# Cross-attention of a decoder layer: one pass with a running maximum, or two passes with the maxima taken first

## The chip, the core and the metric

The kernel runs on one core of a Trainium2 chip. The metric is the device time of one execution in microseconds. TensorE multiplies matrices, VectorE (DVE) and ScalarE (ACT) work on rows, GpSimd (POOL) copies and fills, and SyncE (SP) issues most of the DMA transfers. The engines run their own instruction streams and meet at semaphores.

## What is computed

One decoder layer, cut to what matters here (H = 16 heads of 32, D = 512, 4 batches of 128 queries, 2048 keys each):

```python
q = (layernorm(x) @ Wq.T + bq); k, v = ctx @ Wkv.T + bkv
scores = einsum('bthd,bshd->bhts', q, k * 32 ** -0.5) + attn_bias + where(mask, 0, -inf)
x = x + (softmax(scores) @ v) @ Wo.T + bo            # cross-attention
x = x + self_attention(layernorm(x))                 # clamped
x = x + expert_layer(layernorm(x))                   # 8 experts, 32 rows each and batch
```

The mask lets a query see only keys near the end of the 2048, so most of the 64 chunks of 128 keys are masked as a whole.

## The kernel before, in words

**Which chunks.** A chunk is worked on if its mask has an open key, or if it is the last of its batch. A small table made on the chip lists them; with these inputs it has 11 (four last ones and seven others). Loops with a counter in a register (`Fori`) run over the table, and `chunk_j` and `chunk_b` read its chunk and its batch.

**Prologue.** SP loads x, Wq (`wq_s`), Wk, the first chunk and Wv; ACT loads the rest. Every weight except Wk is split in a rounded part `w_hi` (a copy on ACT) and the remainder `w_lo` (a subtraction on DVE, `split_att`), and a product is three matmuls (hi by hi, hi by lo, lo by hi). The rows of layernorm(x) are turned (`turn_batch`) and split in `tr_hi`, `tr_lo`; `project_t` (L1193) makes the queries `qt` of all batches.

**A chunk** (`chunk`, `softmax_chunk`, with the turned context chunk in `ctx_s`): `k_project` (L1167, 16 full-precision products, in the trace 32 matmuls) makes turned keys in PSUM bank `pk`, DVE adds the bias into `kt_s`. `scores` (L1243, L1248) puts the key bias in the four banks `ps` and adds query by key for 16 heads, four heads side by side in strips of 32 rows. DVE takes the row maxima (L824, two halves) and combines them with those of the chunks before; ACT takes the exponentials (L449, one instruction a head, as each head has its own maximum, with the row sums beside it). TensorE turns the 16 blocks of probabilities (`turn_probs`, L1255), DVE and ACT copy them to `big_b`, `values` (L1268) multiplies by the values, ACT copies the result, TensorE turns it back (`turn_values`, L1276), and DVE rescales `state` and adds. `v_project` (L1177, 12 matmuls) makes the next chunk's values between these steps: chunk t+1's keys, values and scores are made while chunk t is in its softmax.

**Afterwards.** The four batches' results are divided by their row sums, turned, and projected by Wo (`cross_project`, L1193); then come layernorm, self-attention (`project_half`, L1193, begins its queries), the gate, and eight experts, which fill the second half. The change does not touch the experts.

Of the kernel before, what the change touches and what calls it, by code (L numbers as in the profile page):

```python
# [6 lines left out]
ALU = mybir.AluOpType  # L7
# [5 lines left out]
I32 = mybir.dt.int32  # L13
# [23 lines left out]
def decoder_layer(nc, x, ctx_t, key_bias, key_mask, wq, bq, wk, bk, wv, bv, wo, bo,  # L37
                  sq, sbq, sk, sbk, sv, sbv, so, sbo, gate, w1, w2, out):
    with ExitStack() as ctx:
# [11 lines left out]
        ot_s = att_w[:, 6, 0].rearrange("p (k t) -> p k t", k=KC)  # L51
# [5 lines left out]
        ctx_hi, ctx_lo = w_hi[:, 0, :, 0:P], w_lo[:, 0, :, 0:P]  # L57

        x_s = sb("x_s", [P, B, D])
        norm = sb("norm", [P, B, D])  # L60
        gcol = sb("gcol", [P, E])
        qk = sb("qk", [P, 2, B, KC, T])
        qt, kt2 = qk[:, 0], qk[:, 1]
        tr_gate = qt
        state = sb("state", [P, B, D])
        total = sb("total", [P, B, H])
        neg_max = sb("neg_max", [P, B, H])
        sums = sb("sums", [P, H])
# [8 lines left out]
        negm = sb("negm", [P, H])  # L77
        mdiff = sb("mdiff", [P, H])
        alpha = sb("alpha", [P, H])
        norm_c = sb("norm_c", [P, B, H])  # L80
# [5 lines left out]
        table = sb("table", [1, 2 * (NJ + 1) + 2], I32)  # L86
# [11 lines left out]

        tr_hi = early("tr_hi", [P, KC, B * T], F32R)
        tr_lo = early("tr_lo", [P, KC, B * T], F32R)  # L100
        big_a = early("big_a", [P, H, P])
        ctx_s = early("ctx_s", [P, KC, P])
# [4 lines left out]
        values.close()  # L107
        onehot_s = early("onehot_s", [P, B * E * CAP], F32R)
# [12 lines left out]
        kb_m = first("kb_m", [NJ, P])  # L121
        kb_3 = first("kb_3", [NJ, 3, P], BF16)
# [4 lines left out]
        start.close()  # L127
        big_b = early("big_b", [P, H, P])
# [22 lines left out]
        of_group = ctx_s[:, 3].rearrange("p (g m) -> p g m", g=KC)  # L151
# [21 lines left out]
        in_mask, in_wk, in_wv, in_bo, in_sb, in_gate, in_cols = (sem(f"in_{n}") for n in (  # L173
            "mask", "wk", "wv", "bo", "sb", "gate", "cols"))
# [3 lines left out]
        rows_out = sem("rows_out")  # L178
        consts = sem("consts")
        act_ok = sem("act_ok"); place_mm = sem("place_mm")  # L180
        pick_ok = sem("pick_ok"); table_mm = sem("table_mm"); table_ok = sem("table_ok"); rows_ok = sem("rows_ok")
# [32 lines left out]


        TURN_BANKS = [[0, 1, 2, 3], [4, 4, 0, 7], [5, 4, 1, 2], [4] * 4, [1, 2, 3, 1]]
        V2_BANKS = [3, 0, 1, 4]
        CROSS_BANKS = [5, 4, 1, 2]

        def turned(i, b):  # L220
# [1396 lines left out]
```

## Time and profile before

| | us |
|---|---|
| three timed runs | 471.87, 472.13, 474.87 (median 472.13) |
| profiled execution, from its first to its last instruction (its span) | 470.1 |
| first query projection starts | 19.17 |
| scores of chunk 0 start | 32.6 |
| loop over chunks, one turn | 11.6 |
| scores of the last chunk start | 152.0 |
| self-attention queries start (`project_half`) | 179.77 |
| experts start | 261.3 |

No time of its own is given for the profiled execution; its span is 2.0 us under the median of the timed runs, and what lies around the span is in that difference. Times are read from the start of the span. A matmul's end is modelled, so its pace is read from start to start.

### The profile page before, as it was taken

The numbers are of one execution on the slowest core, as the hardware profiler recorded it, in microseconds if no ns is written. First come the engines' busy times: TensorE is split into PE (matmuls) and PEld (weight loads), VectorE is DVE, ScalarE is ACT, GpSimd is POOL, SyncE is SP. The second block draws the span as 40 slices with busy tenths as digits, with TensorE's granted clock in tenths as the row PEclk, the third lists the DMA queues.
The fourth block names the chain that finished last, engine by engine and source line by source line (L and its number), as shares of the span: only waits on it lengthen the run. The fifth ranks groups of instructions, "written<-read, shape, count | busy, mean of one in ns | idle before, by whom it ended". The sixth has DMA issues, their size and how long they took to land.

```text
span 470.1 us, 9681 instructions
## 1 busy us (share of the span) xinstructions
PE 437.7 (93%) x3345; PEld 361.9 (77%) x3345; DVE 371.1 (79%) x513; ACT 295.9 (63%) x609; POOL 79.0 (17%) x89
## 2 busy tenths in 40 slices
PE   1989999999998999989997999999999999999993
PEld 1868888888887779868875877877878787878782
DVE  5986777777778886749887999898989898998853
ACT  1536666666665743466323887777777878787742
POOL 5000000000000013000014250504132230505000
PEclk9999999999999999999999999999999999999998
DMA  7991010000000552520000099999999989998002
GB/s 255 276 342 55 24 24 23 23 23 23 23 23 2 199 205 91 176 93 3 3 1 0 14 392 388 386 386 387 373 345 342 358 305 354 311 386 274 0 0 89
DMA packets 42959, 81.99 MB, mean 174 GB/s; under 512 B 3000, under 2 KB 3128, under 8 KB 42936
## 3 DMA queue, kind: packets, MB, share of 16 engines
q1 hardware_dynamic: 38744, 75.85, 45.6%
q10 hardware_dynamic: 4192, 5.83, 4.0%
q8 instruction: 14, 0.23, 0.2%
q14 instruction: 9, 0.07, 0.0%
HBM read 80.58 MB, written 1.10 MB: 174 GB/s over the span
## 4 chain that ended last, share of the span: by engine, by line
PE 72%; DVE 11%; ACT 9%; DMA 4%; issue 2%; SPq 1%; POOL 0%; DVEq 0%
PE po L1501 19%; PE pk L1501 10%; PE pv L1501 10%; PE pv L1177 6%; ACT big_a L449 5%; PE ps L1193 5%; PE ps L1255 3%; PE pv L1193 3%; PE po L1527 3%; DVE mc L824 3%; PE ps L1248 2%; DMA att_w<-in_wq 2%; PE po L1276 1%; PE pk L1193 1%; DMA rows<-kb 1%
## 5 line engine op out<-in xcount | busy, mean ns | idle before, releaser
L1122 DVE TENSOR_TENSOR w_lo<-att_w,w_hi 128x2048 fp32r<-128x2048 f32 x60 | 137.9, 2306 | 21.6 <-ACT w_hi L643 21.6
L643 ACT CAST w_hi<-att_w 128x2048 fp32r<-128x2048 f32 x60 | 114.9, 1915 | 15.6 <-PE po L1501 15.6
L449 ACT ACTIVATE big_a<-ps,negm 128x128 f32<-128x128 f32 x176 | 62.5, 407 | 21.1 <-DVE negm L827 21.1
L1501 PE MATMUL po<-w_hi,ht_hi 128*128 128x512 f32 x128 | 52.2, 408 | 0.0
L1501 PE MATMUL po<-w_hi,ht_lo 128*128 128x512 f32 x128 | 50.5, 395 | 0.0
L1501 PE MATMUL po<-w_lo,ht_hi 128*128 128x512 f32 x128 | 50.3, 393 | 0.0
L449 ACT ACTIVATION_READ_ACCUMULATOR big_a<-ps,negm 128x1 f32 x176 | 43.4, 247 | 0.0
L1167 PE MATMUL pk<-ctx_s,att_w 128*128 128x128 f32 x352 | 42.5, 279 | 0.4 <-DMA ctx_s<-in_ctx_t 0.4
L1167 PEld LDWEIGHTS pk<-ctx_s,att_w 128*128 128x128 f32 x352 | 40.6, 193 | 2.7 <-issue 1.8
L824 DVE TENSOR_REDUCE mc<-ps 128x8 f32<-128x1024 f32 x22 | 26.9, 1221 | 12.4 <-PE ps L1248 12.4
L1501 PEld LDWEIGHTS po<-w_hi,ht_lo 128*128 128x128 f32 x128 | 24.0, 188 | 6.1
L1501 PEld LDWEIGHTS po<-w_lo,ht_hi 128*128 128x128 f32 x128 | 24.1, 188 | 5.1
L1501 PEld LDWEIGHTS po<-w_hi,ht_hi 128*128 128x128 f32 x128 | 24.1, 188 | 4.9
L387 POOL COPY q_now<-qk 128x512 f32 x10 | 6.3, 626 | 123.8 <-PE ps L1248 123.8
L1501 PE MATMUL pk<-w_hi,xin_hi 128*128 128x512 f32 x64 | 26.3, 411 | 0.0
L1501 PE MATMUL pv<-w_hi,xin_hi 128*128 128x512 f32 x64 | 26.2, 409 | 0.0
L1501 PE MATMUL pk<-w_hi,xin_lo 128*128 128x512 f32 x64 | 25.3, 395 | 0.0
L1501 PE MATMUL pk<-w_lo,xin_hi 128*128 128x512 f32 x64 | 25.2, 394 | 0.0
L1501 PE MATMUL pv<-w_hi,xin_lo 128*128 128x512 f32 x64 | 25.1, 393 | 0.0
L1501 PE MATMUL pv<-w_lo,xin_hi 128*128 128x512 f32 x64 | 25.1, 393 | 0.0
L420 POOL CAST back_now<-state 128x128 fp32r (+1 forms) x8 | 8.6, 1069 | 94.7 <-PE ps L1548 87.8
L1255 PEld LDWEIGHTS ps<-ident,big_a 128*128 128x128 f32 x176 | 21.1, 140 | 4.3
(300 smaller groups left out, 990.9 us busy)
## 6 DMA issues: line engine op xcount, KB each, us to landing
att_w<-in_w SPq DMA_DIRECT2D x64, 1024.0 KB, 6.9
ctx_s<-in_ctx_t SPq DMA_DIRECT2D x11, 256.0 KB, 2.6
x_s<-in_x SPq DMA_DIRECT2D x4, 256.0 KB, 3.4
att_w<-in_wq SPq DMA_DIRECT2D x1, 1024.0 KB, 8.3
att_w<-in_wk SPq DMA_DIRECT2D x1, 1024.0 KB, 11.1
att_w<-in_wv SPq DMA_DIRECT2D x1, 1024.0 KB, 6.2
att_w<-in_sv ACTq DMA_DIRECT2D x1, 1024.0 KB, 8.3
att_w<-in_wo ACTq DMA_DIRECT2D x1, 1024.0 KB, 10.3
```

The source lines that it names most:

```text
L420: g.tensor_copy(back_now[:], back[:, bass.ds(e, 1), :].rearrange("p a n -> p (a n)")).then_inc(back_staged, 1)
L449: ins = a.activation(big_a[:, h], ps[:, c, g * P:(g + 1) * P], ACT.Exp, bias=negm[:, h:h + 1], accum_out=sums[:, h:h + 1])
L643: a.copy(w_hi[:, i % SLOTS], att_w[:, i]).then_inc(hi_ok, 1)
L824: v.tensor_reduce(mc[:, hs], ps[:, 2 * half:2 * half + 2].rearrange("p c (g k) -> p (c g) k", k=P), AX.X, ALU.max).then_inc(loop_dve, 1)
L1122: v.tensor_tensor(w_lo[:, i % SLOTS], att_w[:, i], w_hi[:, i % SLOTS], ALU.subtract).then_inc(lo_ok, 1)
L1167: ins = mm(pk[:, g * P:(g + 1) * P], wk_s[:, k, g * P:(g + 1) * P], ctx_s[:, k], start=k == 0, stop=k == KC - 1)
L1177: ins = mm(pv[:], c[:, k], w[:, 1, k], start=k == 0 and c is ctx_hi and w is w_hi, stop=k == KC - 1 and c is ctx_lo, skip_group_check=True)
L1193: ins = mm(dst, l, r, start=n == 0, stop=n == len(pairs) - 1, skip_group_check=True)
L1248: ins = mm(ps[:, c, g * P:(g + 1) * P], q_now[r, g], kt_s[r, g], start=False, stop=True, skip_group_check=True)
L1255: ins = nc.tensor.transpose(ps[:, c, g * P:(g + 1) * P], big_a[:, c * KC + g], ident[:])
L1501: ins = mm(dst, l, r, start=start and i == 0, stop=i == len(terms) - 1, skip_group_check=True)
L1527: ins = nc.tensor.transpose(po[:, 1, c * P:(c + 1) * P], h_s[:, q % 2, c * P:(c + 1) * P], ident[:])
```

## The change

1. The maxima come first. Each batch's last chunk is known without the table: its context is loaded early to `ctx_last`, its keys are made early (`last_keys`) and stay in SBUF (`kt_last`), and its scores' maxima are taken before the loops. Then a first loop over the other chunks (n = 7) makes keys, scores and maxima only. It writes each chunk's keys to DRAM (`kept_kt`).
2. The maxima are placed in rows (`shift_rows`), turned by TensorE and kept as `neg_t`.
3. A second loop reads the keys back, makes the scores turned (keys on the rows, `scores_t`) with the maximum already subtracted, and takes four exponentials of 512 columns with the key bias as a column `kb_now`. Probabilities come out in the layout that `values` needs, so that `turn_probs`, `turn_values`, the rescaling and their copies are gone. Row sums are matmuls with `of_group` beside the values.
4. After the second loop each batch's last chunk follows, and the row sums are inverted and spread by matmuls (`spread_cross`), as self-attention does.
5. The keys' bias is added on ACT (`keys_out`), `ctx_k` and `bias3` are copies of what is loaded, Wk and the first batch's last chunk are loaded ahead of Wq, Wo and the others are loaded by SP, and the biases come in one transfer.

The core of the diff (cut; lines of TensorE, ACT and DVE):

```diff
         @block.scalar
+            act.wait_ge(in_cols, 16)
+            last_keys(0)
             split_att(0)
             for b in range(B):
                 transposed(0, b)
...
+            with act.Fori(0, n) as t:
+                act.wait_ge(kept, t * 16 + 16)
+                act.wait_ge(k_mm, 2 * t + 1)
+                keys_out(kt_s, pk, 0, 2).then_inc(k_out, 1)
+                act.wait_ge(k_mm, 2 * t + 2)
+                keys_out(kt_s, pv, 2, 4).then_inc(k_out, 1)
+                act.wait_ge(k_out, 2 * t + 2)
+                act.dma_start(kept_kt[bass.ds(t, 1)].rearrange("a p (k n) -> (a p) k n", k=KC), kt_s[:]).then_inc(kept, 16)
...
         @block.vector
+            def lower(nm, i):
...
+                v.tensor_reduce(mc[:], ps[:].rearrange("p c (g k) -> p (c g) k", k=P), AX.X, ALU.max).then_inc(max_ok, 1)
+                dve.wait_ge(max_ok, 2 * i + 1)
+                v.scalar_tensor_tensor(nm, mc[:], -1.0, nm, ALU.mult, ALU.min).then_inc(max_ok, 1)
+            for b in range(B):
+                dve.wait_ge(sl_mm, b + 1)
+                lower(neg_max[:, b], b)
+                if b == 1:
+                    split_att(2)
...
         @block.tensor
+            with pe.Fori(0, n) as t:
+                pe.wait_ge(ctx_k_ok, t + 1)
+                k_project(pk, ctx_k, 0, 2).then_inc(k_mm, 1)
+                k_project(pv, ctx_k, 2, 4).then_inc(k_mm, 1)
+                pe.wait_ge(bias_ok, t + 1)
+                pe.wait_ge(q_staged, t + 1)
+                pe.wait_ge(max_ok, 2 * t + (2 * B - 1))
+                pe.wait_ge(k_out, 2 * t + 1)
+                scores(bias3, q_now, kt_s, 2 * t + 2).then_inc(s_mm, 1)
...
+            with pe.Fori(0, n) as t:
+                pe.wait_ge(kt_in, t * 16 + 16)
+                pe.wait_ge(staged2, 2 * t + 2)
+                pe.wait_ge(p_ok, t + 1)
+                scores_t(neg_now, q_now, kt_s).then_inc(st_mm, 1)
+                pe.wait_ge(ctx_lo_ok, t + 2)
+                pe.wait_ge(v_out, t + 1)
+                v_project(pv[:], 0).then_inc(v_mm, 1)
+                pe.wait_ge(p_ok, t + 2)
+                pe.wait_ge(acc_ok, t + 1)
+                values(0).then_inc(pv_mm, 1)
```

TensorE, the turn of a chunk in the loop before: `pk` holds keys, `pv` values, `ps` scores and turned probabilities, `po` the output; of the twelve value matmuls the first three stand for all.

```order
L1255 MATMUL ps<-ident,big_a 128x128 [waits p_ok]
L1255 MATMUL ps<-ident,big_a 128x128 x3
L1177 MATMUL pv<-w_hi 128x512
L1177 MATMUL pv<-w_lo,w_hi 128x512
L1177 MATMUL pv<-w_hi,w_lo 128x512
...
L1243 MATMUL ps<-bias,ones 128x512 [waits pt_act,pt_dve]
L1243 MATMUL ps<-bias,ones 128x512 x3
L1248 MATMUL ps<-kt_s,q_now 128x128 x16
```

and what stands in the first and in the second loop now:

```order
L1229 MATMUL pk<-ctx_k,att_w 128x128 [waits ctx_k_ok]
L1229 MATMUL pk<-ctx_k,att_w 128x128 x7
L1229 MATMUL pv<-ctx_k,att_w 128x128 x8
L1363 ISA [waits q_staged,bias_ok]
L1364 REGISTER_ALU [waits max_ok]
...
L1295 MATMUL ps<-kt_s,q_now 128x128 x8
...
L1295 MATMUL ps<-kt_s,q_now 128x128 [waits k_out]
...
L1312 MATMUL ps<-neg_now,ones 128x512 [waits p_ok]
L1312 MATMUL ps<-neg_now,ones 128x512 x3
L1316 MATMUL ps<-q_now,kt_s 128x128 x16
```

The turns of probabilities are gone; scores stand twice, and the first loop's end with a wait for keys.

DVE ahead of the first loop, in the changed kernel (`ps` is the one set of score banks, `x_s` the rows of x, `ctx_k` the copy that TensorE's first loop waits for); before, DVE had no such row, since a chunk's maxima stood beside TensorE's next projections:

```order
L852 TENSOR_TENSOR w_lo<-big_a,w_hi 128x4x128 [waits cl_hi_ok] x2
L855 TENSOR_TENSOR x_s<-x_s,bo_b 128x512 [waits in_rows]
L855 TENSOR_TENSOR x_s<-x_s,bo_b 128x512 x3
L867 TENSOR_REDUCE mc<-ps 128x16 [waits sl_mm,dchain]
L869 SCALAR_TENSOR_TENSOR neg_max<-mc,neg_max 128x16 [waits max_ok]
...
L808 TENSOR_TENSOR w_lo<-att_w,w_hi 128x2048 [waits att_hi_ok]
...
L880 COPY ctx_k<-ctx_s 128x512 [waits ctx1_in,kept]
```

Four reductions, each behind scores in the same banks, now stand between TensorE's last scores and its first loop. ACT's start, in the changed kernel (`qk` takes the keys of the first last chunk):

```order
L538 ACT_TABLE_LOAD [waits kl_mm]
L538 ACTIVATE qk<-pk,cols 128x128 [waits in_cols]
L538 ACTIVATE qk<-pk,cols 128x128 x3
L524 CAST w_hi<-att_w 128x2048 [waits in_wq]
L528 CAST tr_hi<-ps 128x4x128 [waits tr_mm0] x4
```

The table load and the split of Wq moved behind the wait for the first keys' matmuls (`kl_mm`).

## Rows read from the trace of the kernel before

**Rows 1.** The page, busy time of each engine and share of the span.

```profile
PE 437.7 (93%) x3345; PEld 361.9 (77%) x3345; DVE 371.1 (79%) x513; ACT 295.9 (63%) x609; POOL 79.0 (17%) x89
```

**Rows 2.** Timeline of TensorE: start, duration, what [idle before it and releaser].

```profile
38.25 3.73 PE L1167 MATMUL pk<-ctx_s,att_w 128*128 128x128 f32 x32
41.73 0.48 PE L1177 MATMUL pv<-w_hi 128*128 128x512 f32 x1
...
46.59 0.40 PE L1243 MATMUL ps<-bias,ones 32*128 32x512 bf16 x4
...
47.80 1.08 PE L1268 MATMUL po<-big_b,v_s 128*32 128x128 f32 x32
48.81 3.84 PE L1167 MATMUL pk<-ctx_s,att_w 128*128 128x128 f32 x32
52.95 0.66 PE L1276 MATMUL po<-ident,att_w 128*128 128x128 f32 x4 [0.30 <-ACT att_w L460]
...
58.20 0.40 PE L1243 MATMUL ps<-bias,ones 32*128 32x512 bf16 x4
```

**Rows 3.** Windows after TensorE's wait at 30.7; the last but two column: granted clock.

```profile
32.60:34.60 2.00, 2.00 (x37) 1.77 (x38) 1.98 (x1) 0.00 (x0) 0.00 (x0) 0.63 1.05 406
34.60:36.40 1.80, 1.80 (x5) 1.41 (x6) 1.64 (x4) 0.00 (x0) 0.72 (x1) 0.50 0.99 331
```

**Rows 4.** Timeline of TensorE, the waits and starts outside the loop.

```profile
19.17 0.48 PE L1193 MATMUL ps<-tr_hi,w_hi 128*128 128x512 f32 x1
...
30.26 0.40 PE L1193 MATMUL ps<-tr_lo,w_hi 128*128 128x512 f32 x1
32.58 0.40 PE L1243 MATMUL ps<-bias,ones 32*128 32x512 bf16 x4 [1.93 <-DMA bias<-rows]
...
179.77 0.36 PE L1193 MATMUL pk<-tr_hi,w_hi 128*128 128x256 f32 x1
...
207.16 1.17 PE L1365 MATMUL ps<-qk 32*128 32x128 f32 x32 [1.33 <-DVE qk L972]
```

**Rows 5.** Timeline of TensorE: a projection of 12 matmuls, spread sums, values with sums.

```profile
156.42 0.48 PE L1193 MATMUL pv<-w_hi,tr_hi 128*128 128x512 f32 x1
...
159.29 1.03 PE L1255 MATMUL ps<-ident,big_a 128*128 128x128 f32 x8
...
226.17 1.05 PE L1394 MATMUL po<-kt_s,q_now 128*128 128x128 f32 x8
227.15 0.43 PE L1383 MATMUL po<-big_b,v_s 128*32 128x128 f32 x8
...
229.03 0.50 PE L1193 MATMUL pv<-w_hi,tr_hi 128*128 128x512 f32 x1
```

**Rows 6.** Groups by line on DVE and ACT: busy us, mean ns | idle before.

```profile
L824 DVE TENSOR_REDUCE mc<-ps 128x8 f32<-128x1024 f32 x22 | 26.9, 1221 | 12.4 <-PE ps L1248 12.4
L721 DVE TENSOR_TENSOR w_lo<-att_w,w_hi 128x2048 fp32r<-128x2048 f32 x7 | 16.0, 2286 | 2.5 <-ACT w_hi L438 2.5
L841 DVE TENSOR_TENSOR state<-state,alpha 128x512 f32 x11 | 7.5, 684 | 0.1
L987 DVE RECIPROCAL kt_s<-po 128x128 f32<-128x128 f32 x2 | 1.9, 954 | 0.2 <-PE po L1386 0.2
...
L449 ACT ACTIVATE big_a<-ps,negm 128x128 f32<-128x128 f32 x176 | 62.5, 407 | 21.1 <-DVE negm L827 21.1
...
L549 ACT ACTIVATE qk<-po,cols 128x512 f32<-128x512 f32 x2 | 1.4, 690 | 1.5 <-PE po L1193 1.5
```

**Rows 7.** Timeline of ACT at the start.

```profile
4.74 1.28 ACT L438 ACT_TABLE_LOAD   x1 [4.74 <-issue]
11.12 1.90 ACT L438 CAST w_hi<-att_w 128x2048 fp32r<-128x2048 f32 x1 [5.09 <-DMA att_w<-in_wq]
```

**Rows 8.** DMA issues: KB each, median us from issue to landing.

```profile
ctx_s<-in_ctx_t SPq DMA_DIRECT2D x11, 256.0 KB, 2.6
...
rows<-kb SPq DMA_DIRECT2D x1, 48.0 KB, 5.8
```

More of the change, by code:

```diff
@@ new lines, in last_keys, with split_last, exponents @@
+            def last_keys(b):
+                act.wait_ge(kl_mm, b + 1)
+                keys_out(kt_last[:, b], pk, 0, KC).then_inc(kl_out, 1)
+            def split_last(b):
+                act.wait_ge(in_last, 48)
+                a.copy(ctx_part(w_hi, b), ctx_last[:, b]).then_inc(cl_hi_ok, 1)
+            def exponents(bias):
+                for c in range(STRIPS):
+                    ins = a.activation(big_a[:, c * KC:(c + 1) * KC].rearrange("p g n -> p (g n)"), ps[:, c], ACT.Exp, bias=bias)
+                return ins
@@ new lines, in scores @@
+            def scores(rows, queries, keys, waits):
+                for c in range(STRIPS):
+                    r = slice(c * DH, (c + 1) * DH)
+                    mm(ps[:, c].rearrange("p (g k) -> p g k", g=KC), ones3[r], rows[r].unsqueeze(1).broadcast_to([DH, KC, P]),
+                       start=True, stop=False, skip_group_check=True)
+                for g in range(KC):
+                    if g == 2 and waits is not None:
+                        pe.wait_ge(k_out, waits)
+                    for c in range(STRIPS):
+                        r = slice(c * DH, (c + 1) * DH)
+                        ins = mm(ps[:, c, g * P:(g + 1) * P], queries[r, g], keys[r, g], start=False, stop=True, skip_group_check=True)
+                return ins
@@ new lines, in last_scores, with scores_t @@
+            def last_scores(b):
+                pe.wait_ge(kl_out, b + 1)
+                if b == 0:
+                    pe.wait_ge(bias_last_in, 64)
+                    pe.wait_ge(q_out, KC)
+                else:
+                    pe.wait_ge(max_ok, 2 * b - 1)
+                scores(bias_last[:, b], qt[:, b], kt_last[:, b], None).then_inc(sl_mm, 1)
+            def scores_t(rows, queries, keys):
+                for c in range(STRIPS):
+                    r = slice(c * DH, (c + 1) * DH)
+                    mm(ps[:, c], ones3[r], rows[r], start=True, stop=False, skip_group_check=True)
+                for g in range(KC):
+                    for c in range(STRIPS):
+                        r = slice(c * DH, (c + 1) * DH)
+                        ins = mm(ps[:, c, g * P:(g + 1) * P], keys[r, g], queries[r, g], start=False, stop=True, skip_group_check=True)
+                return ins
@@ L1224, in _ @@
+            pe.wait_ge(consts, 10)
+            pe.wait_ge(in_wk, 16)
+            last_keys(0)
+            for b in range(B):
+                turn_batch(0, b)
+            pe.wait_ge(act_ok, 1)
+            mm(pv[0:NJ, 0:1], tri[:], idx[:, 7:8], start=True, stop=True).then_inc(table_mm, 1)
+            last_keys(1)
+            pe.wait_ge(tr_lo_ok[0], B)
+            pe.wait_ge(att_lo_ok, 1)
+            project_t(2, banks[0:4], q_mm)
             pe.wait_ge(pick_ok, 1)
@@ L1297, in _ @@
-            for b in range(B):
-                turn_batch(0, b)
-            pe.wait_ge(in_wk, 16)
-            k_project(0)
-            pe.wait_ge(tr_lo_ok[0], B)
-            pe.wait_ge(att_lo_ok, 1)
-            project_t(2, banks[0:4], q_mm)
-            pe.wait_ge(q_out, 4)
-            scores(0)
-            pe.wait_ge(att_lo_ok, 2)
-            for k in range(KC):
-                v_project(0, k)
-            chunk(0, False)
-            with pe.Fori(1, prev) as t:
-                chunk(t, True)
@@ L1350, in _ @@
             pe.wait_ge(tr_lo_ok[2], B)
-            project_half(1, banks[4:8], 1, q2_mm)
+            project_half(1, q2_dst, 1, q2_mm)
             pe.wait_ge(v2_out, B - 1)
```

830 lines of the change are left out of this document (431 added, 399 removed).

## The prediction

> **What bounds the kernel now.** I read the page of the profile first: TensorE is busy 93% of the span [rows 1]. Then its timeline in the loop over chunks. From the scores at 46.59 to the next at 58.20 are 11.61 us [rows 2], and TensorE's only recorded wait there is 0.30, for ACT's copy of the last output; by starts it is more, since 32 key matmuls started at 38.25 let the next group start at 41.73, so 3.48 us after, while those of 48.81 are followed at 52.95 only: 0.66 us lost a turn. I take 0.2 more as lost before the scores, where the turned probabilities must first be copied from the same banks. So TensorE's own work is 10.7 of 11.6 us, and no change of the softmax can gain more than 0.9 us a chunk unless it takes work from TensorE. Outside the loop TensorE waited 1.93 us for the key bias at 30.7 [rows 4], and afterwards its clock was granted at 0.63 and then 0.50 of full speed until 36.4 [rows 3]: of its two levels the lower, 1.2 GHz, for some 3.8 us, in which half the work is done: 1.9 us lost. A wait of 1.33 at 205.8 [rows 4] had no such cost.
>
> **TensorE's work, old and new.** Prices from start to start: keys 3.48, scores 1.21 (46.59 to 47.80), values 1.01 [rows 2]; a projection of 12 matmuls 2.87, a spread of sums 0.98, values with sums 1.88 [rows 5]. The change removes 16 turns of probabilities (about 1.5, by the rest of the 11.61) and four turns of the output (0.4), makes the scores twice (+1.21) and adds the sums to the values (+0.87). A chunk costs 3.48 + 1.21 + 2.87 + 1.21 + 1.88 = 10.65, as before. What it can gain are the loop's waits; what it can lose are new waits where one loop became a prologue, two loops, a middle and a closing part. I follow TensorE through them.
>
> **Prologue, up to the queries.** The first keys need Wk and a chunk, as many bytes as went before Wq's landing at 11.1 [rows 7]; the four column loads and a broadcast that ran beside are gone, so I take 10.3 (9.5 to 11.1). The first products run at the low clock, 3.48 + 1.9: keys done at 15.7. ACT, which before had split Wq from 11.1, now stands behind them: a table load of 1.28, then of 4 x 0.27 + 0.1 = 1.2 for the keys (four 128-column activations; 407 ns each [rows 6], issued faster), then the split of 1.90 [rows 7], to 20.3 with handovers. DVE's remainder takes 2.29 and four turned remainders 2.5 (0.68 each alone, some 0.6 in a row [rows 6]): the query projection starts at 25.2, against 19.17 [rows 4]. TensorE has turned x and made the second keys by 22.0 and waits 3.2 us. It then takes 11.3 (30.26 + 0.23 less 19.17) + 1.9 for the clock: 38.4.
>
> **Prologue, up to the first loop.** Scores of batch 0 wait for the last queries on ACT: 39.4 to 40.6. Nine small instructions of DVE for the table hold TensorE till 40.9; third keys till 44.4. DVE meanwhile does two remainders (1.3) and adds bo to x (four, 2.5), and only then the maxima: 2048 columns cost twice 1.22 less one start, 2.3 [rows 6], to 47.0. The scores' banks are free then: a wait of 2.6. At the low clock those scores take 2.4, to 49.5, and the fourth keys end at 53.7 (0.7 late); scores to 54.9. DVE reduces and splits the third weight in between, and reduces batch 2 till 57.4: a wait of 2.6, slow scores to 59.9. Then the first loop waits for the last reduction and the copy to ctx_k: 0.25 + 2.3 + 0.2 + 0.5, to 63.2, a wait of 3.3.
>
> **First loop.** Keys 3.48; their last result is out 0.25 later, ACT needs 0.27 + 0.37 and two handovers for the second half, so the second half of the scores starts at 4.55 and ends at 5.1. DVE's 0.4 + 0.2 + 2.3 + 0.2 and POOL's copy fit beside. Behind ACT's wait for `kept` stands the first half of the keys' copy. It is not waited for if the DRAM write lands within 3.5 us of its issue (5.1 + 3.48 less 4.55 and the copy). 256 KB in the other direction land in 2.6, 48 KB of `rows` took 5.8 behind other loads [rows 8]; I take the nearer row, 2.6, and keep 5.8, by which a turn is 7.0 and the time 12 more, for the range. Seven turns of 5.1 and 1.9 for the clock: 100.8. The Trainium skill (DMA: Bandwidth & Descriptors, Anatomy of one DMA) says that completion can take surprisingly long when the target is HBM; the trace of before has no unhindered write of this size in the loop to test it. By the page's fit of 2.0 us and 436 GB/s I get, as an estimate, 2.6 us and an unchanged sum.
>
> **Between the loops.** Three value projections 8.6, 16 turns of 0.41 are 1.65, a wait of 0.95 for DVE (last maximum, 19 small instructions, a remainder, two copies of 0.68), and 0.9 for the keys read back, whose load is queued behind three weights of 1 MB: 12.1, to 112.9.
>
> **Second loop.** 1.21 + 2.87 + 1.88 = 5.96, I take 6.0. ACT's four exponentials (0.69 each alone [rows 6], 2.2 together) end 2.5 after the scores, under the 2.87 of the projection; DVE's copy of the values ends 0.95 after the values, under the next scores' 1.21. Seven turns: 42.0, to 154.9. Both loops together give 11.1 a chunk, 0.5 less than before: 3.6 us gained.
>
> **Closing part.** TensorE's work up to `project_half`: 4 scores 4.8, a projection 2.9, 4 values 7.5, 4 spreads 3.9, 4 + 2 projections 17.2, 3 turns 1.2: 37.6. Its waits, by DVE's order, are 1.05 and 0.55 for the first sums (0.9 to add, 0.95 for the reciprocal [rows 6]), 0.6 for batch 1's remainder, 2.0 before batch 2's projection (scale, ACT copy, remainder), 1.0 for batch 3's reciprocal, 1.3 for the remainder of the queries' weight: 6.5. So 44.1, to 199.0 (179.77 before [rows 4]): +19.2. Self-attention's rest and the experts keep their order and their loads are early enough, at 0; in the worst case later loads of Wsq would add a few us, which I do not expect. So span 489.3, and with the 2.0 between span and median 491.3. I take 490, as one of the four slow stretches may not come or may be shorter.
>
> **The clock.** Rows 3 and 4 show that 1.93 us of waiting were enough. The new waits at 22.0, 44.4, 54.9 and 59.9 are 3.2, 2.6, 2.6 and 3.3, longer. They cost 1.9 + (1.2 + 0.7) + 1.2 + 1.9 = 6.9. The Trainium skill (TensorE: Matmul & The Clock Gate, What's actually happening) calls the lower rate the default that activity lifts, with a phase that is not the kernel's; whether each wait is caught is then not settled by its length alone. The trace agrees for the wait it has.
>
> **Rivals.** (A) The waits come, but the clock stays up at all four. For it: 1.33 us did nothing; against it: 1.93 did. 490 - 6 = 484. (B) The DRAM write sets the first loop, as priced: 490 + 12 = 502; half of it, with a landing at 4.6, gives 495. Against it: the queue is empty there but for 256 KB a turn. (C) Faster: TensorE is never kept waiting, in prologue, middle or closing part, and its work alone sets the end. That takes away 3.2 + 1.0 + 0.3 + 2.6 + 2.6 + 3.3 + 0.95 + 0.9 + 6.5 = 21.4 and the 6.9 of the clock: 463. It decides at the reductions: if DVE's 2.3 us were hidden under a projection, as before, it would be so; against it, there is one set of score banks and the next scores stand behind the reduction. For half of it, 476. (D) The small instructions and handovers, which I estimated, are 10% dearer everywhere: 494; this lies in the range of the first.
>
> **How the numbers follow.** All four stretches or three of them slow, 490: 0.68 (its own range 484 to 496). A, 484 (479 to 486): 0.18. B, 502 or part of it: 0.08. C, or enough of it for no loss: 0.06, of it 0.04 faster by over 1%, under 467.4, and 0.02 within 1%. About 1% of 472.13, 4.7 us, is what a measurement of this kernel can tell from no change. A is above 476.9, so it is slower. Slower is 0.68 + 0.18 + 0.08 = 0.94; I give 0.03 of it to the same for a sum of small errors: slower 0.91, same 0.05, faster 0.04. The range from 479 to 498 leaves out C and the worse half of B.
>
> **What would show it.** The changed profile should have: queries' projection starting near 25 with a table load of 1.3 after the first keys; three waits of 2.5 to 3.3 on TensorE for L867 or L880, each followed by a granted clock of 0.5; a first loop of 5.1 a turn with no wait for DMA; a second of 6.0; DVE's and ACT's busy time lower; `project_half` near 197 to 199; then 290 us as before. The prediction is wrong if the first loop waits for `kept`, if the second is set by ACT or DVE, or if the stage between the last scores and `project_half` is hidden.

## The result, and the profile after

The changed kernel takes 496.95 us (median of 4 runs, 492.29 to 498.92), the kernel before 472.66 in the runs beside it: a ratio of 1.051, 95% interval 1.0469 to 1.0551, so slower by 5%. The forecast was 490 with a range from 479 to 498, so the median lies 1 us inside the upper end, and one run in four outside it. The profiled execution took 498.92, and its span is 497.2, where the forecast had a span of 489.3.

The page of the changed kernel, busy time of each engine (answers to [rows 1]):

```profile
PE 450.0 (91%) x3906; PEld 373.0 (75%) x3906; DVE 338.5 (68%) x422; ACT 264.1 (53%) x319; POOL 93.2 (19%) x116
```

DVE has 32.6 us less to do and ACT 31.8, and the time is longer all the same. TensorE is busy for 12.3 us more, most of it work at half rate. This is what a share of busy time can't tell: the two engines that were relieved were not the ones that ended last.

TensorE's waits, engine and line waited for, then total us, times, longest:

```profile
PE ps L1288 <- DVE mc L867: 4.7, 2, 2.5
PE pk L1229 <- DVE ctx_k L880: 3.9, 1, 3.9
PE ps L1312 <- DMA kt_s<-kept_kt: 3.1, 1, 3.1
PE ps L1248 <- DVE tr_lo L802: 2.6, 1, 2.6
```

The first is made of 2.18 at 46.7 and 2.52 at 56.8, the two reductions that stand between one set of scores and the next. All were forecast, as 2.6 twice, 3.3, 0.9 and 3.2. The windows in which TensorE's clock was low (windows of the changed kernel; busy time of each engine, then the granted clock, the last but two column; answers to [rows 3]):

```profile
26.50:32.70 6.20, 6.16 (x15) 4.80 (x16) 2.65 (x3) 2.02 (x4) 0.00 (x0) 0.50 0.27 103
48.90:53.60 4.70, 4.69 (x52) 4.48 (x53) 3.16 (x4) 0.00 (x0) 0.00 (x0) 0.64 0.01 3
64.80:70.30 5.50, 5.49 (x25) 5.49 (x26) 0.06 (x1) 0.63 (x2) 0.00 (x0) 0.50 0.19 48
118.00:121.00 3.00, 3.00 (x38) 2.63 (x39) 0.51 (x1) 0.70 (x2) 0.56 (x2) 0.52 0.31 91
265.00:268.50 3.50, 3.50 (x9) 2.79 (x10) 2.03 (x5) 0.00 (x0) 0.55 (x1) 0.53 0.00 0
```

0.50 is the lower of the two levels, 1.2 GHz. Each window follows a wait, and costs its length times what is missing to 1.00: 3.1, 1.7, 2.7, 1.4 and 1.6 us. The fourth runs on a little, to 121.5. A short stretch behind the wait that ends at 59.29 (0.73 from 59.3 to 61.0) costs 0.5 more. The last lies in the part that the change does not touch, behind 16 recorded matmuls of 8 columns, four of 128 and a wait of 0.50 us.

A turn of each loop, from TensorE's timeline (start, duration; answers to [rows 2]):

```profile
77.84 2.05 PE L1229 MATMUL pk<-ctx_k,att_w 128*128 128x128 f32 x16
79.73 1.95 PE L1229 MATMUL pv<-ctx_k,att_w 128*128 128x128 f32 x16
81.64 0.39 PE L1288 MATMUL ps<-bias,ones 32*128 32x512 bf16 x4
81.87 1.26 PE L1295 MATMUL ps<-kt_s,q_now 32*128 32x128 f32 x32
83.06 2.05 PE L1229 MATMUL pk<-ctx_k,att_w 128*128 128x128 f32 x16
...
125.60 0.39 PE L1312 MATMUL ps<-neg_now,ones 32*128 32x512 bf16 x4
125.82 1.06 PE L1316 MATMUL ps<-q_now,kt_s 32*128 32x128 f32 x32
129.76 0.43 PE L1323 MATMUL po<-big_a,v_s 128*32 128x128 f32 x8
...
131.64 0.39 PE L1312 MATMUL ps<-neg_now,ones 32*128 32x512 bf16 x4
```

The first loop turns in 83.06 - 77.84 = 5.22 us, the second in 131.64 - 125.60 = 6.04. Together 11.26, against 11.61 before: 0.35 a chunk gained, in a loop whose softmax is gone.

The rest of the milestones, from TensorE's timeline, with the waits in brackets (answers to [rows 4]):

```profile
11.78 5.68 PE L1229 MATMUL pk<-big_a,att_w 128*128 128x128 f32 x32 [11.78 <-DMA big_a<-in_ctx_t]
...
26.54 0.79 PE L1248 MATMUL ps<-tr_hi,w_hi 128*128 128x512 f32 x1 [2.61 <-DVE tr_lo L802]
...
41.68 0.40 PE L1288 MATMUL ps<-bias_last,ones 32*128 32x512 bf16 x4 [0.32 <-ACT qk L583]
...
64.81 3.78 PE L1229 MATMUL pk<-ctx_k,att_w 128*128 128x128 f32 x16 [3.88 <-DVE ctx_k L880]
...
117.98 0.55 PE L1312 MATMUL ps<-neg_now,ones 32*128 32x512 bf16 x4 [3.12 <-DMA kt_s<-kept_kt]
...
190.36 0.50 PE L1248 MATMUL ps<-w_hi,tr_hi 128*128 128x512 f32 x1 [1.72 <-DVE tr_lo L979]
...
205.60 0.38 PE L1248 MATMUL pk<-tr_hi,w_hi 128*128 128x256 f32 x1 [1.06 <-DVE w_lo L808]
```

The last of these rows is `project_half`, at 179.77 before. The change costs 25.8 us up to there, and 1.3 behind it (497.2 - 205.6 against 470.1 - 179.77), which the 1.6 of the window at 265 covers. So four questions were open: is it the waits, and each of them for the reason that I had read; is it the clock, and does the clock follow the waits; how near was the DRAM write to setting the first loop; and do the waits account for everything, so that a kernel without them is no slower than before?

### The profile page after: what moved, and what is told of

It is laid out like the page before. It is cut to its first block, busy times and chain, and to the rows that moved or that the text cites. A ratio compares the mean times of both kernels' runs of the same rounds, so it can differ in the third digit from the quotient of the medians.

```text
span 497.2 us, 10365 instructions
## 1 busy us (share of the span) xinstructions
PE 450.0 (91%) x3906; PEld 373.0 (75%) x3906; DVE 338.5 (68%) x422; ACT 264.1 (53%) x319; POOL 93.2 (19%) x116
## 4 chain that ended last, share of the span: by engine, by line
PE 79%; DVE 11%; DMA 3%; ACT 3%; issue 2%; SPq 1%; DVEq 0%; POOL 0%; ACTq 0%
PE po L1621 18%; PE pv L1248 9%; PE pk L1621 9%; PE pv L1621 9%; PE ps L1248 6%; PE pk L1229 5%; PE po L1647 3%; PE pv L1229 2%; PE po L1323 2%; PE ps L1295 2%; PE ps L1316 2%; DVE mc L867 2%; PE po L1326 2%; DMA big_a<-in_ctx_t 2%; PE pk L1248 1%
## 5 line engine op out<-in xcount | busy, mean ns | idle before, releaser
L1229 PE MATMUL pk<-big_a,att_w 128*128 128x128 f32 x128 | 18.5, 313 | 12.5 <-DMA big_a<-in_ctx_t 11.8
L867 DVE TENSOR_REDUCE mc<-ps 128x16 f32<-128x2048 f32 x11 | 25.2, 2290 | 4.8 <-PE ps L1295 4.8
L1229 PEld LDWEIGHTS pk<-big_a,att_w 128*128 128x128 f32 x128 | 17.8, 227 | 12.9 <-issue 12.8
L552 ACT ACTIVATE big_a<-ps,kb_now 128x512 f32<-128x512 f32 x28 | 17.0, 689 | 17.3 <-PE ps L1316 17.3
L1621 PE MATMUL pv<-w_hi,xin_lo 128*128 128x512 f32 x64 | 25.2, 394 | 0.0
L929 DVE TENSOR_TENSOR w_lo<-ctx_s,w_hi 128x512 fp32r<-128x512 f32 x9 | 6.2, 692 | 26.9 <-ACT w_hi L560 26.9
L500 POOL COPY x_now<-qk 128x512 f32 x7 | 16.2, 2308 | 38.3 <-PE pv L1621 38.3
L503 POOL TENSOR_TENSOR xin_lo<-x_now,xin_hi 128x512 fp32r<-128x512 f32 x7 | 23.0, 3288 | 0.6
```

Source lines behind the costliest of these rows:

```text
L500: g.tensor_copy(x_now[:], now).then_inc(x_now_ok, 1)
L503: g.tensor_tensor(xin_lo[:], x_now[:], xin_hi[:], ALU.subtract).then_inc(xin_staged, 1)
L552: ins = a.activation(big_a[:, c * KC:(c + 1) * KC].rearrange("p g n -> p (g n)"), ps[:, c], ACT.Exp, bias=bias)
L867: v.tensor_reduce(mc[:], ps[:].rearrange("p c (g k) -> p (c g) k", k=P), AX.X, ALU.max).then_inc(max_ok, 1)
L1229: ins = mm(dst[:, g * P:(g + 1) * P], wk_s[:, k, g * P:(g + 1) * P], chunk[:, k], start=k == 0, stop=k == KC - 1)
L1621: ins = mm(dst, l, r, start=start and i == 0, stop=i == len(terms) - 1, skip_group_check=True)
```

## The experiments

**Keeping TensorE busy in its waits.** Nothing is moved; matmuls that nobody reads stand in the waits.

```diff
+            def keep_busy(n):
+                for _ in range(n):
+                    mm(po[:, 0, 0:P], ident[:], ident[:], start=True, stop=True, skip_group_check=True)
...
             last_keys(1)
+            keep_busy(9)
             pe.wait_ge(tr_lo_ok[0], B)
...
             last_keys(2)
+            keep_busy(7)
             last_scores(1)
             last_keys(3)
             last_scores(2)
+            keep_busy(8)
             last_scores(3)
+            keep_busy(14)
...
             pe.wait_ge(neg_t_ok, B)
+            keep_busy(11)
             with pe.Fori(0, n) as t:
```

> The changed kernel, with 9, 7, 8, 14 and 11 matmuls that nobody reads (128x128 of the identity by itself, into a bank that is free) where TensorE waits 2.61, 2.18, 2.52, 3.88 and 3.12 us. If the waits bring the low clock (my account), the granted clock stays at 1.0 to the end of the first turn of the second loop, and the time falls by what the slow stretches lost: 3.1 from 26.5 to 32.7, 1.7 from 49 to 54, 0.4 at 59.3, 2.6 from 64.8 to 70 and 1.6 from 118 to 121, so 9.4: some 487.5. The runs should also lie closer together than 492.3 to 498.9. Rival: the clock falls for a reason that is not the waits (a rhythm of its own, or the load); then the slow stretches stay, and the time is 497 or somewhat more, since surplus matmuls then delay the next group.

Measured: 489.12 us (487.58 to 490.18), ratio 1.0342 (1.0285 to 1.0398), 7.8 less than the changed kernel. Its windows where the clock had been low:

```profile
26.10:38.40 12.30, 12.01 (x55) 9.37 (x55) 3.03 (x6) 4.27 (x8) 0.00 (x0) 1.00 0.15 56
45.70:50.60 4.90, 4.89 (x68) 4.75 (x68) 3.58 (x4) 0.00 (x0) 0.00 (x0) 1.00 0.00 0
54.40:63.40 9.00, 8.35 (x96) 7.98 (x96) 3.15 (x5) 0.62 (x2) 0.00 (x0) 1.00 0.13 30
110.40:113.40 3.00, 2.93 (x44) 2.53 (x45) 0.08 (x1) 1.57 (x3) 1.17 (x2) 1.00 0.39 107
```

All at 1.00, and the runs lie within 2.6 us of each other where the changed kernel's spread over 6.6; the mean granted clock of the four is 0.989 to 0.996, that of the changed kernel's four 0.965 to 0.977. `project_half` starts at 196.50, 9.1 earlier, against 9.4 expected. More work, less time: the clock follows the waits, and cost the changed kernel some 8 of its 24 us.

**The same in the kernel before.** Eight such matmuls in its wait of 1.93 us.

```diff
             project_t(2, banks[0:4], q_mm)
+            keep_busy(8)
             pe.wait_ge(q_out, 4)
             scores(0)
```

> The kernel before, with 8 matmuls that nobody reads in its wait of 1.93 us at 30.7. By my account of the clock the granted clock then stays at 1.0 from 32.6 to 36.4 and the time from the first scores to the loop's first falls from 14.0 to 12.1: 471 where the kernel before has 473. Rival: the low clock there has nothing to do with the wait, and the stretch stays at 14.0.

Measured: 472.07 (10 runs), ratio 0.999 (0.9961 to 1.0019). The mechanism came as expected, the gain did not. In its profile the clock is 1.00 where it was 0.57, and from the first scores, at 33.99, to the loop's first, at 46.41, are 12.4 us, not 14.0:

```profile
32.11 1.95 PE L1223 MATMUL po<-ident 128*128 128x128 f32 x16
33.99 0.39 PE L1247 MATMUL ps<-bias,ones 32*128 32x512 bf16 x4
...
46.41 0.40 PE L1247 MATMUL ps<-bias,ones 32*128 32x512 bf16 x4
```

But the unread matmuls last to the very start of the scores, and the profile shows no wait behind them; in this execution the projection also ended 1.6 us later than in [rows 4]. How much of the 1.6 us they gave back by lasting too long the profile can't say. In the medians 0.5 us of gain is left, and the interval goes from 1.8 us less to 0.9 more, so that the 2 us expected are all but excluded and a smaller gain is not. This execution also has a slow stretch that the one of [rows 3] doesn't, from 250 to 254 us (0.57), behind a wait of 1.45 in the part that nobody changed. So the control shows the link between wait and clock a second time, and that filler of the wait's full length is worth nothing that these runs can tell; that it must end sooner is a reading of this profile, and wasn't tried.

**The first chunk's copies ahead of the last reduction.**

```diff
             for b in range(B):
+                if b == B - 1:
+                    dve.wait_ge(kept, 16)
+                    dve.wait_ge(ctx1_in, 16)
+                    next_chunk().then_inc(ctx_k_ok, 1)
+                    dve.wait_ge(bias_in, 64)
+                    next_bias().then_inc(bias_ok, 1)
                 dve.wait_ge(sl_mm, b + 1)
                 lower(neg_max[:, b], b)
```

> The changed kernel, with the copies of the first chunk and its bias (ctx_k, bias3) ahead of the fourth reduction on DVE instead of behind it. If the wait of 3.88 us ahead of the first loop is DVE's order alone, the keys of the loop start right behind the last scores: 3.9 less, and the 2.6 that the low clock cost in the first turn come back as well where the clock doesn't fall at 59.3 already; between 3.9 and 6.5 less, 491 to 493. Rival: the chunk's load or its bias (over DRAM) is what is late there, and the copy was only next to it: then the wait stays in another place and the time is within 1 us of 497.

Measured: 490.76 (489.3 to 493.75), ratio 1.0393 (1.0328 to 1.0458): 6.2 less, in the upper half of what was expected. The wait is gone (TensorE's timeline; the keys of the first loop now follow the last scores):

```profile
56.45 0.40 PE L1289 MATMUL ps<-bias_last,ones 32*128 32x512 bf16 x4 [2.51 <-DVE mc L867]
...
57.96 3.37 PE L1230 MATMUL pk<-ctx_k,att_w 128*128 128x128 f32 x16
...
63.05 0.40 PE L1289 MATMUL ps<-bias,ones 32*128 32x512 bf16 x4
```

From the fourth last scores to the loop's first are 6.6 us, against 11.9 in the changed kernel (59.29 to 71.19). There DVE had (timeline of the changed kernel):

```profile
60.99 2.29 DVE L867 TENSOR_REDUCE mc<-ps 128x16 f32<-128x2048 f32 x1 [1.64 <-PE ps L1295]
63.32 0.17 DVE L869 SCALAR_TENSOR_TENSOR neg_max<-mc,neg_max 128x16 f32<-128x16 f32 x1
64.33 0.43 DVE L880 COPY ctx_k<-ctx_s 128x512 f32<-128x512 f32 x1 [0.84 <-issue]
```

So the 3.9 us were one instruction of 0.43 us standing behind one of 2.29 (and 0.84 of `issue`, where DVE by its order reads the number of turns), on an engine that is busy for 68% of the span.

**The weights' loads behind the second loop.**

```diff
             load_chunk(first_j, ctx2_in)
-            load_att(sq_s, sq, in_sq)
-            load_att(sk_s, sk, in_sk)
-            load_att(so_s, so, in_so)
-            sp.dma_start(gate_s[:], ...).then_inc(in_gate, 16)
...
+            load_att(sq_s, sq, in_sq)
+            load_att(sk_s, sk, in_sk)
+            load_att(so_s, so, in_so)
+            sp.dma_start(gate_s[:], ...).then_inc(in_gate, 16)
             sp.wait_ge(v_out, n + 2)
```

> The changed kernel, with the loads of the three weights of 1 MB and of the gate behind the second loop on SP's queue, not ahead of its first read of keys. If the keys' first read was late because it stood behind 3 MB, the wait of 3.12 us ahead of the second loop falls to under 0.6 and its slow clock (1.6) goes: 4 less, 493. Rival: the read waits for the end of the last write to DRAM and for the copy of V's chunk, not for the queue; then the wait stays over 2 us. A second rival: the weights, now issued near 157, come late in the closing part (the split at 195), which would show as a wait for DMA there and cost up to 5.

Measured: 493.71 (490.53 to 497.17), ratio 1.046 (1.0397 to 1.0523), 3.2 less in the median. The runs overlap with those of the changed kernel, so the stage is the better witness: from the turned maxima to the second loop's first scores are 5.9 us (105.67 to 111.61) against 8.5 (109.49 to 117.98), and the loop behind them takes 42.4 against 43.9. That is 4.1, as expected. The first read of the keys, issued behind the weights at 112.64, took 5.1 us to its landing in the changed kernel; here it is issued at 108.83 and takes 2.4. Where it was late there is now this:

```profile
111.61 0.40 PE L1312 MATMUL ps<-neg_now,ones 32*128 32x512 bf16 x4 [0.56 <-POOL neg_now L474]
```

The closing part takes 43.74 us, as before the move (43.72), so the weights, issued some 45 us later, still come in time.

**DVE's additions early.**

```diff
             split_att(1)
+            for b in range(2, B):
+                dve.wait_ge(cl_hi_ok, b - 1)
+                v.tensor_tensor(ctx_part(w_lo, b), ...).then_inc(cl_lo_ok, 1)
+            dve.wait_ge(in_rows, 32)
+            for b in range(B):
+                ins = v.tensor_tensor(x_s[:, b], x_s[:, b], bo_b[:], ALU.add)
+            link(ins)
             dve.wait_ge(table_mm, 2)
```

(and away from behind the table)

> The changed kernel, with DVE's two remainders of the last chunks and the four additions of bo (3.75 us) put into its idle time of 12 us before 41.2, ahead of the table. Then the first reduction starts at 42.9 instead of 46.5 and ends before the next scores are due: TensorE's wait of 2.18 goes, and so does the slow stretch from 49 to 54: 2.2 + 1.7 = 3.9 less, 493. Rival: DVE's split of the third weight, which stands between the second and the third reduction, takes the place of the first one as what is late, so that the later waits grow by what is gained: within 1 us of 497.

Measured: 491.32 (490.76 to 496.28), ratio 1.0415 (1.0339 to 1.0491), 5.6 less, more than expected. The wait of 2.18 is gone, and from the first last scores to the first loop are 20.2 us (37.68 to 57.85) against 23.1: 2.9, less than the 3.9 forecast for it. What came on top is in part a chance of the clock. The same wait of 2.6 us stands ahead of the query projection as before, but here the clock did not fall:

```profile
25.30:31.30 6.00, 5.95 (x26) 4.81 (x27) 5.91 (x9) 2.20 (x5) 0.00 (x0) 1.00 0.37 139
```

**Wq first.** The order of the kernel before at the start.

```diff
+            load_att(wq_s, wq, in_wq)
             load_att(wk_s, wk, in_wk)
             load_last(0)
-            load_att(wq_s, wq, in_wq)
...
-            last_keys(0)
             split_att(0)
             for b in range(B):
                 transposed(0, b)
-            last_keys(1)
+            last_keys(0)
             split_att(1)
...
-            pe.wait_ge(in_wk, 16)
-            last_keys(0)
             for b in range(B):
                 turn_batch(0, b)
...
-            last_keys(1)
+            pe.wait_ge(in_wk, 16)
+            last_keys(0)
             pe.wait_ge(tr_lo_ok[0], B)
             pe.wait_ge(att_lo_ok, 1)
             project_t(2, banks[0:4], q_mm)
...
-            nc.tensor.transpose(pk[:, 0:NJ], kb_m[:], ...)
+            nc.tensor.transpose(po[:, 0, 0:NJ], kb_m[:], ...)
+            last_keys(1)
             last_scores(0)
```

> The changed kernel with the order of the kernel before at its start: Wq is loaded ahead of Wk and the first last chunk, ACT splits it before it touches keys, TensorE turns x before the first keys, and the second keys come behind the query projection. If the keys put ahead of Wq are what made the start late, the query projection starts at 19 to 20, as before, and the scores of batch 0 at 35 to 36, not at 41.7: 6 less, 491. Rival: Wk and the chunk, now behind Wq, come so late that the first keys hold the projection; then it starts at 21 or more and the gain is under 4.

Measured: 484.9 (484.55 to 489.69), ratio 1.0301 (1.0243 to 1.0358): 12.0 less, twice what was expected. TensorE's timeline:

```profile
18.39 0.51 PE L1248 MATMUL ps<-tr_hi,w_hi 128*128 128x512 f32 x1 [0.71 <-DVE tr_lo L802]
...
34.10 0.40 PE L1288 MATMUL ps<-bias_last,ones 32*128 32x512 bf16 x4
35.50 3.81 PE L1229 MATMUL pk<-big_a,att_w 128*128 128x128 f32 x32
39.24 0.39 PE L1288 MATMUL ps<-bias_last,ones 32*128 32x512 bf16 x4
```

The projection starts at 18.39, and the first last scores 7.6 us earlier, since the wait of 2.6 ahead of the projection is 0.7 and its slow stretch is gone. The rest is what I had not counted: the second keys now lie between the projection and the first scores, and DVE makes its additions beside them; the second last scores follow the third keys with no wait (39.24), so that the 2.18 and its slow stretch are gone as well.

**How near the DRAM write is.** Less of it, and twice as much:

```diff
-    act.dma_start(kept_kt[...], kt_s[:]).then_inc(kept, 16)
+    act.dma_start(kept_kt[...][:, 0:1], kt_s[:, 0:1]).then_inc(kept, 16)
```

> The changed kernel, where only the first quarter of each chunk's keys (64 KB, not 256) is written to DRAM and read back; three quarters of the keys of the second loop are left out, with the same instructions. In the changed kernel ACT waits 3.7 to 3.8 us of every turn of the first loop for the write, and copies the keys 0.06 us before the scores want them. If the write doesn't set the loop, its turn stays at 5.21 and only ACT's wait shrinks. If it does (the rival), the turn falls to 5.0 or less.

```diff
     act.dma_start(kept_kt[...], kt_s[:]).then_inc(kept, 16)
+    act.dma_start(kept_kt2[...], kt_s[:]).then_inc(kept, 16)
```

> The changed kernel, where each chunk's keys are written to DRAM twice, into two places (512 KB a turn). The write now lands 3.6 to 4.3 us after its issue, with at most 0.2 us to spare by my reading. Then every 0.1 us of later landing shows: I expect a landing some 0.6 to 1.2 later and a turn of 5.7 to 6.3, 3.5 to 7.5 us more in all. Rival: there is slack of over 1 us (as I had forecast less than 1), and the turn stays under 5.3.

The first of them leaves out three quarters of the second loop's keys, so that it tells about the first loop's pace alone. Measured, one run each, 493.56 and 497.63 us; a single run says little, and the turns are read from the traces. The groups of transfers by KB and us to landing, of the changed kernel and then of the smaller write:

```profile
kept_kt<-kt_s ACTq DMA_DIRECT2D x7, 256.0 KB, 3.6
kt_s<-kept_kt SPq DMA_DIRECT2D x7, 256.0 KB, 2.5
```

```profile
kept_kt<-kt_s ACTq DMA_DIRECT2D x7, 64.0 KB, 2.8
kt_s<-kept_kt SPq DMA_DIRECT2D x7, 64.0 KB, 1.8
```

With the small write the turn is 5.21 (80.12 to 85.33), as in the changed kernel, and ACT waits again for TensorE. So the write doesn't set the loop. But it just doesn't, as ACT's row in the changed kernel shows:

```profile
80.96 0.62 ACT L538 ACTIVATE kt_s<-pk,cols 128x128 f32<-128x128 f32 x2 [3.83 <-DMA kept_kt<-kt_s]
```

The copy ends at 81.58, and the scores that read it start at 81.64; in the turn where it ends latest, at 92.14, they start at 92.20, and that turn still takes 5.21 (88.27 to 93.48). With two writes the starts of the turns are 68.62, 74.34, 79.55, 85.39, 90.60 and 96.35: every other turn takes 5.7 to 5.8, and the mean is (96.35 - 68.62) / 5 = 5.55, 0.34 more. That is less than the 0.5 to 1.1 I expected, and more than the rival's, so both were off: there is some slack, of a few tenths, and then the write shows.

**The four moves together.** Wq first, the copies first, the read first, the additions early.

> The changed kernel with the four moves that each gained by themselves: Wq first at the start, DVE's additions early, the first chunk's copies ahead of the fourth reduction, the weights' loads behind the second loop. If the gains are of different waits and add up: from 484.9 (Wq first alone) the wait ahead of the first loop goes (3.9) with some 1.0 of its slow clock, and the wait ahead of the second falls by 2.2 with 1.0 of slow clock: 476.8, between 475 and 479. The wait of 2.5 between the third and the fourth last scores must stay, since TensorE has nothing there. Rival: waits grow elsewhere on DVE, which is as long as before in this stretch: then 480 or more.

Measured: 479.55 (477.12 to 481.77), ratio 1.0166 (1.0121 to 1.0211), 0.6 above the range from 475 to 479, and under the rival's 480. The profiled execution is the fastest one, and in it no stretch up to `project_half` is slow: `project_half` starts at 184.89, 5.1 behind the kernel before. The gains don't add up (6.2 + 3.2 + 5.6 + 12.0 = 27.0, measured 17.4), since the early additions and the early Wq remove the same wait, and several of them the same slow stretches.

**Work in place of filler.** The values of batch 3's last chunk in the wait between the third and fourth last scores, those of the first chunk ahead of the turned maxima, and two moves in the closing part:

```diff
             last_scores(2)
+            v_project(po[:, 0], 3).then_inc(vl_mm, 1)
             last_scores(3)
...
-            v_project(pk[:], 3).then_inc(vl_mm, 1)
-            v_project(pv[:], 2).then_inc(vl_mm, 1)
+            v_project(pk[:], 2).then_inc(vl_mm, 1)
+            pe.wait_ge(ctx_lo_ok, 1)
+            v_project(pv[:], 0).then_inc(v_mm, 1)
...
             cross_project(1)
+            spread_cross(2)
             last_values(3)
-            spread_cross(2)
...
+            split_att(4)
             cross_output(3)
-            split_att(4)
```

> The kernel of the four moves, with work put into its remaining waits: the values of batch 3's last chunk are projected between the third and fourth last scores (into a free bank), those of the first chunk ahead of the turned maxima; the spread of batch 2's sums stands ahead of batch 3's values, and DVE's split of the queries' weight ahead of the last residual. If waits are all that holds the changed kernel back: 2.5 + 1.5 of clock in the prologue, 1.7 + 1.1 in the closing part, 6 to 7 less than the four moves: 470 to 471, faster than or the same as the kernel before (472.6). Rival: the turned maxima, with less work ahead of them, are what is late in the middle: a wait of 1 to 3 us there, and 472 to 474.

Measured: 477.41 (476.07 to 479.45), ratio 1.0118 (1.0077 to 1.0159), 2.1 less than the four moves in the medians, with intervals that overlap, and not the 6 to 7 expected. The rival was right, and more than right: it had a wait of 1 to 3 us and 472 to 474. TensorE's timeline in the middle:

```profile
99.52 0.61 PE L1314 MATMUL ps<-neg_now,ones 32*128 32x512 bf16 x4 [4.03 <-POOL neg_now L474]
```

The middle is set by a chain: the last reduction, 19 small instructions on DVE, the turned maxima, four copies on ACT, and the copy to `neg_now` on POOL. The four moves have 13.1 us from the last scores of the first loop to the first of the second (85.70 to 98.77), this kernel 13.8 (85.71 to 99.52), with one projection of 2.87 less on TensorE. Work taken out of a place where it was cover is no gain, and the new wait brought a slow stretch again (0.56, 0.50 and 0.80 in three windows of 3 us from 98.0). In the two profiled executions the closing part is 3.4 us shorter than with the four moves (40.35 against 43.75), the second loop 2.6 longer (44.95 against 42.37), the middle 0.7, and `project_half` starts at 184.82 where it was 184.89.

**The closing moves, and filler in the one wait left.** The four moves, `keep_busy(9)` ahead of `last_scores(3)`, and the last two hunks of the diff above; the projections of values are back in their places.

> The kernel of the four moves, with the two moves of the closing part (the spread of batch 2's sums ahead of batch 3's values, DVE's split of the queries' weight ahead of the last residual) and 9 unread matmuls in the wait between the third and the fourth last scores. The projections of values stay where the changed kernel has them, so that they cover the chain from the last maximum to neg_now. If the closing waits and the clock are as I read them: 1.7 + 1.1 + up to 0.7 in the closing part, and 1 to 3 in those runs in which the clock fell: 479.6 - 3.5 - 1.5 = 474.6, between 473 and 477, and at best even with the kernel before. Rival: what is taken from one closing wait comes back in the next one on DVE, and the time stays at 478 or more.

Measured: 473.21 (472.22 to 476.31, 12 runs), kernel before 472.58 (470.52 to 475.0) beside it: ratio 1.0016, 95% interval 0.9993 to 1.0038. That is in the range expected (473 to 477), and nothing is left of the 5% that a measurement could tell. Its profiled execution, at 475.68 one of the slower ones, still starts `project_half` 2.7 us behind the kernel before (182.44). The kernel before got no such moves in its own prologue or behind its loop; what they would bring there wasn't tried, so the two are even only as they stand.

## Why the prediction was right, and where it was off

- **The direction and its reason held.** The loops were forecast to give 0.5 us a chunk and gave 0.35; the waits around them were forecast as what decides, and the last kernel, which removes most of them and keeps both passes, is as fast as the one before. This also answers rival C, that TensorE might never wait: as the change is written, it waited at every place named but one (0.3 us for the small instructions of the table), and its price of 463 was too low. With 94% of its span busy TensorE still needs 473.
- **Up to the queries**: forecast 25.2, measured 26.54. The first keys start at 11.78, not 10.3. This is 0.7 beyond the upper bound of 9.5 to 11.1, for the chunk took 9.4 us from issue to landing among the other loads.
- **The clock**: the mis-sized term. Forecast 6.9 up to `project_half`, lost 9.1 to 9.4: 3.1 where I had 1.9 for the projection, and 1.5 at the start of the second loop where I had none, because I had priced that wait at 0.9. I took the slow stretches as long as the one in [rows 3], and that one as 1.9 us lost, which by its own two windows is 1.6 (2.0 x 0.37 + 1.8 x 0.50); the longest here, 6.2 us, lost 3.1. Rival A, that the clock stays up at all four waits, fell; but at single waits, in single executions, it does stay up. So the 0.68 for "all four or three of them" had the right case, and that this execution met all four is in part chance.
- **The wait for the kept keys**: 3.12, forecast 0.9. I had named the three weights on the queue ahead of the read, and priced them too low. Moving them took the wait away, so the cause was right: behind them the first read took 5.1 us to its landing, the seven reads 2.5 in the median.
- **Before the first loop**: forecast from the first last scores to the loop 23.8 (39.4 to 63.2), measured 23.1 (41.68 to 64.81). The reductions stood where the order had put them.
- **Keys cost more than I took**: 3.77 from start to start in every turn, not 3.48. The row that I read this from, 38.25 to 41.73 in [rows 2], was the fast one; in the same group the loop's own keys need from 48.81 to 52.95 with 0.30 of wait, and I booked the rest as a wait that the change could gain. The first loop's turn was thus 5.21 for 5.1, and the gain of both loops 0.35 for 0.5 a chunk.
- **Rival B, the DRAM write**: it does not set the loop. I chose 2.6 us of landing and kept 5.8 as the other end; it is 3.6. The limit that I worked out, 3.5 us from the issue, is about where it stands: ACT waits for the write in six turns of seven (3.7 to 4.0 us), and ends its copy 0.06 us before it is needed. So by the letter one sign of being wrong came, "if the first loop waits for `kept`": ACT does. The path to the end does not run through this wait, as the small write shows, whose turn is no shorter; but the forecast's picture of a loop with no wait for DMA was wrong.
- **The closing part**: 44.1 forecast, 43.72 measured, with waits of 0.96, 0.47, 0.29, 1.72, 0.72 and 1.06 for the forecast 1.05, 0.55, 0.6, 2.0, 1.0 and 1.3. The second of them is for ACT's exponentials, not for sums.
- **The rest**: forecast without change, measured 1.3 more, by the slow stretch at 265. It is chance, and common: of the thirteen profiled executions nine have a slow stretch somewhere between 240 and 277 us, and four have none (the kernel before, that with busy waits, that with Wq first and the four moves). In the kernel with busy waits the part from `project_half` to the end is 290.0 (486.5 - 196.50). So the run that the forecast was built on was a lucky one there, by some 1.3 us.

Added up, in us: 1.3 to the queries, 1.0 for the clock in their projection, 0.7 less to the first loop, 1.5 in it, 2.0 between the loops, 1.9 in the second, 0.4 less in the closing part, and 1.3 behind it make 7.9, the difference between the forecast span of 489.3 and the measured one of 497.2.

Which of the chip's rules held: the Trainium skill (TensorE: Matmul & The Clock Gate, What's actually happening) describes a lower default rate that activity lifts, with a phase of its own. The traces here agree. In the profiled executions, one for each kernel, the wait of 2.6 ahead of the query projection was followed by a low clock in four of the six that had it, that of 2.18 ahead of the second last scores in two of five, that of 2.5 ahead of the fourth last scores in seven of eight (in six of these one of 3.88 follows), and that of 2.8 to 3.2 ahead of the second loop in four of five; a wait of 1.95 there, with the small write, was followed by one too. Here are two windows behind such waits in the kernel with the copies first, at full rate, where the changed kernel has 0.64 and 0.52:

```profile
47.60:52.60 5.00, 4.94 (x68) 4.78 (x68) 3.67 (x4) 0.00 (x0) 0.00 (x0) 1.00 0.01 3
109.60:112.60 3.00, 2.98 (x44) 2.56 (x45) 0.53 (x1) 1.62 (x3) 1.17 (x2) 1.00 0.31 93
```

This is also why the changed kernel's times spread over 6.6 us. What stays open is what decides in a single execution. Shown is that waits of 1.9 us and more can bring a low clock, and that up to `project_half` filling them took it away. That only such waits bring it is not shown: in the part behind, slow stretches came where the last waits were 0.2 to 1.5 us and matmuls of 8 columns had gone before, as at 265.

## What to carry to other kernels

When a change takes work from engines that are not the bound, count what it does to the bound's waits: each phase that it adds (a prologue, a second loop, a middle, a closing part) begins with a wait for what the phase before it left, and here these seams cost far more than the 0.35 us a chunk that the loops gained. Look in the written order for a short instruction, or a small transfer, that the bound waits for and that stands behind a long one that it doesn't: four such moves, the start's order among them, took back 17 us, and none touched the arithmetic. And price a wait on TensorE twice, once for itself and once for the half rate that may follow it; but don't count on filler as long as the wait itself, and fill it with real work only where that work was not cover somewhere else.

## What was not expected of the hardware

- The keys' write to DRAM, on ACT's queue, takes 1.0 to 1.1 us longer to its landing than their read on SP's: 3.6 against 2.5 for 256 KB, 2.8 against 1.8 for 64 KB. The Trainium skill (DMA: Bandwidth & Descriptors, Anatomy of one DMA) warns that completion is slow when the target is HBM; the trace agrees with the direction, and by its fit I had estimated 2.6. The page gives that fit for transfers that GpSimd issues, and these were issued by ACT and SP. Write and read differ here in queue as well as in target, so that the target makes the difference is not shown.
- A second write of 256 KB on the same queue cost the loop only 0.34 us a turn in the mean, not a whole landing, and only in every other turn.
- POOL took about 2 us between the semaphore that it waits for ahead of the second loop and its copy, as the kernel with work in its waits shows: ACT's last copy of the maxima ends at 96.26, and POOL's next copy starts at 98.21, with `issue` as what its idle time ended with. Two values are read into registers there. That the reading takes the time is argued, not shown: I have not tried to read them earlier.
